# Carrying the second LayerNorm's transpose by VectorE blocks and SBUF transfers instead of TensorE, in an attention and feed-forward kernel

## Chip, cores and metric

One NeuronCore of one Trainium2 chip runs the whole program. The metric is the device time in microseconds (us) of one execution, and a lower time is better. A profiled execution of the same program gives the trace.

## The reference, cut to what matters

For each of 16 batches, `x` has 512 rows of 512 features and the context has 77 rows of 512.

```python
def block(x, ctx):
    h = layernorm(x)                                  # first LayerNorm
    sim = (h @ w1)[:, None] + (ctx @ w2)[None] + (h * w3) @ ctx.T + b
    hq = softmax(sim, axis=1) @ ctx
    hc = softmax(sim.max(axis=1)) @ h
    x = x + concat([h, hq, h * hq, h * hc]) @ W_qv + b_qv
    h2 = layernorm(x)                                 # second LayerNorm
    u = h2 @ W1 + b1
    q = u + (cos(th) * wr + sin(th) * wi) * wi * sin(th + 0.1 * u) * 0.1
    return x + relu(q) @ W2 + b2
```

`W1` is 512 x 2048 and `W2` 2048 x 512.

## The kernel before, in words

**Products.** Each fp32 matrix is held as a rounded high part and a low part, and each product is three matmuls (high x high, high x low, low x high; `three`, lines 500 to 502). A matmul of the feed-forward part has 128 partitions and 512 moving columns. `T[:, par]` holds the rows of one batch turned, so that features lie on the partitions: `T[:, par, 0]` is the high part, `T[:, par, 1]` the low part, each 4 chunks of features by 512 rows. The two values of `par` alternate from batch to batch.

**Order of the work.** The loop `body(b)` runs over 16 hidden tiles f = 0 to 15 of the feed-forward part of batch b and interleaves with them the attention of batch n = b + 1. All five engines have their own hand-written program with the same loop, and semaphores join them. On TensorE step f is `hidden(b, f)` (line 546, 12 matmuls into the PSUM tile `hid`) and then `second(b, f - 3)` (12 matmuls into `acc`). ScalarE reads `hid` in two passes (L846, L849), VectorE reduces the phase (L1168, L1170), ScalarE takes the sine (L859), VectorE adds it (L1160), and the ReLU is split into high and low parts (L855, L1174). Attention of the next batch: similarities in step 3, row and column maxima in steps 4 and 5, the turned probabilities in step 8, the products with `W_qv` in steps 10 and 11 (NA = 10). After these VectorE adds the result to `X` and takes the statistics of the second LayerNorm (`attention_and_stats`, line 1268), and GpSimd turns these into a reciprocal deviation (`deviation_second`, line 1552).

**The second LayerNorm's transpose.** In steps NA + 3 = 13 and NA + 4 = 14 the normalized rows are turned. `norm_second` (line 1276) on VectorE writes 128 rows to one of two buffers of `xin`; `tr_second` (line 599) on TensorE makes four 128 x 128 transposes through the identity into `mis` (L586, in `transpose_rows`, line 581); `turned_high` (line 764) on ScalarE rounds them from PSUM into the high part of `T`; `turned_low` (line 1065) on VectorE subtracts that from PSUM for the low part. `hidden(b + 1, 0)` waits for the last low part (`t2_lo`).

**The first LayerNorm's rows** come already turned from memory (`full`). The mean and deviation of each row are stored to DRAM and loaded back spread over the partitions (`spread_stats`, line 348, into `mean_bc` and `e_bc`); VectorE subtracts and multiplies (`center`, `scale`, L1047 and L1053), ScalarE and VectorE split the result (`spread_high`, `spread_low`, L771 and L1027).

**Queues.** SyncE issues the loads of inputs, the stores, `spread_stats` and `ctx_load` (line 381, seven transfers to `ctx_raw` and `tmp_w`), in program order. GpSimd issues the weight loads (512 KB each). In batch 0 the weights are split on the way and stored to DRAM, and later batches load them split, so in batch 0 ScalarE, VectorE and SyncE have more to do.

**The opening** (`attention_first` of each engine) splits `W_qv`'s second quarter, multiplies all context rows by it in ten groups (`rows_in`, `high_parts`, `low_part`, `multiply`, `product_add`, `product_out`), and works the attention of batch 0 between them. Its second LayerNorm is turned on TensorE too.

## Time and profile before

| what | us |
| --- | --- |
| median of 3 runs | 1970.97 (1969.54 to 1971.58) |
| the profiled execution, its own time | 1970.5 |
| its span in the trace | 1968.7 |
| TensorE busy | 1948.3 |
| VectorE busy | 1387.2 |
| ScalarE busy | 988.9 |
| GpSimd busy | 389.4 |

The span runs from the first instruction to the last in the trace, 1.8 us less than the execution's own time. In the rows a matmul's own duration is longer than the distance to the next one, since matmuls overlap; the distance between starts is what one costs. PE is TensorE, PEld its weight load, DVE VectorE, ACT ScalarE, POOL GpSimd, and SPq SyncE's DMA issues. A row with "x2" merges that many instructions. In square brackets, or behind a bar, stands the idle time before the instruction and what ended it. L12 is line 12 of the kernel before.

### The profile page before, as it was taken

Reading aid. Unit: us, or ns where it says so; the run is one execution under the profiler, and the core shown is the slowest. Engines: PE = TensorE matmul, PEld = TensorE weight load, DVE = VectorE, ACT = ScalarE, POOL = GpSimd, SP = SyncE. Lnnn points to the kernel's source line nnn. Section 1 sums busy time; section 2 is a strip of 40 time slices with the busy share of each in tenths; the row PEclk is TensorE's granted clock in tenths of the full one; section 3 lists DMA queues with packets and bytes.
Section 4 is the critical chain, followed back from the end, with each engine's and each line's share of the span. In section 5 each row is a group of like instructions: output and inputs, shape, how many; then the busy total and the mean of one; then the engine's idle time right before and its main releaser. Section 6 shows DMA issues by size and latency. Waiting matters only on the chain.

```text
span 1968.7 us, 24691 instructions
## 1 busy us (share of the span) xinstructions
PE 1948.3 (99%) x8807; PEld 1598.2 (81%) x8807; DVE 1387.2 (70%) x2405; ACT 988.9 (50%) x1676; POOL 389.4 (20%) x834
## 2 busy tenths in 40 slices
PE   8899999999999999999999999999999999999999
PEld 6678888888888888888888888888888888888887
DVE  6888776767777676776767767676776767767554
ACT  4574635536355363644636355363653636446343
POOL 1122212121211212112121211212112121121210
PEclk9999999999999999999999999999999999999999
DMA  8476947577474775747667485764747757476473
GB/s 247 166 266 240 291 145 224 182 212 222 152 224 144 243 220 160 237 145 222 203 189 226 138 236 166 225 221 155 232 134 242 222 166 231 146 221 181 146 216 119
DMA packets 140849, 391.73 MB, mean 199 GB/s; under 512 B 21876, under 2 KB 34856, under 8 KB 138808
## 3 DMA queue, kind: packets, MB, share of 16 engines
q0 software_dynamic: 83568, 304.29, 49.6%
q1 hardware_dynamic: 57016, 85.83, 14.0%
q8 instruction: 71, 1.16, 0.2%
q14 instruction: 50, 0.41, 0.1%
q10 hardware_dynamic: 144, 0.04, 0.0%
HBM read 351.83 MB, written 38.27 MB: 198 GB/s over the span
## 4 chain that ended last, share of the span: by engine, by line
PE 92%; DVE 3%; ACT 2%; DMA 1%; issue 1%; SPq 0%; DVEq 0%; ACTq 0%
PE acc L500 17%; PE acc L502 17%; PE acc L501 17%; PE hid L502 11%; PE hid L500 11%; PE hid L501 11%; PE mis L586 1%; PE acc L508 1%; PE acc L509 1%; PE mis L508 1%; PE mis L509 1%; PE mis L500 1%; PE mis L502 1%; PE mis L501 1%; DMA ph<-in_ctx_turned 1%
## 5 line engine op out<-in xcount | busy, mean ns | idle before, releaser
L500 PE MATMUL acc<-ws,act 128*128 128x512 f32 x1024 | 402.8, 393 | 1.7 <-DVE act L1174 1.7
L500 PE MATMUL hid<-T,w1s 128*128 128x512 f32 x1024 | 402.8, 393 | 0.4 <-ACT h L849 0.3
L502 PE MATMUL acc<-ws,act 128*128 128x512 f32 x1024 | 399.2, 390 | 0.0
L502 PE MATMUL hid<-T,w1s 128*128 128x512 f32 x1024 | 399.0, 390 | 0.0
L501 PE MATMUL acc<-ws,act 128*128 128x512 f32 x1024 | 398.7, 389 | 0.0
L501 PE MATMUL hid<-T,w1s 128*128 128x512 f32 x1024 | 398.7, 389 | 0.0
L1168 DVE TENSOR_SCALAR kk<-ph 128x512 f32<-128x512 f32 x256 | 108.8, 425 | 329.5 <-ACT ph L846 329.5
L855 ACT ACTIVATE act<-h 128x512 fp32r<-128x512 f32 x256 | 162.0, 633 | 351.7 <-DVE h L1160 330.3
L846 ACT ACTIVATE ph<-hid,hbias 128x512 f32<-128x512 f32 x256 | 175.8, 687 | 285.3 <-PE hid L502 285.0
L1509 POOL DMA_DIRECT2D ws<-w2x_dram x240 | 127.5, 532 | 556.2 <-PE acc L502 546.7
L1174 DVE SCALAR_TENSOR_TENSOR act<-h,act 128x512 fp32r<-128x512 f32 x256 | 176.0, 688 | 74.4 <-ACT act L855 73.1
L500 PEld LDWEIGHTS acc<-ws,act 128*128 128x128 f32 x1024 | 192.4, 188 | 41.7 <-DVE act L1174 2.5
L500 PEld LDWEIGHTS hid<-T,w1s 128*128 128x128 f32 x1024 | 192.3, 188 | 41.7 <-issue 1.2
L502 PEld LDWEIGHTS hid<-T,w1s 128*128 128x128 f32 x1024 | 192.2, 188 | 40.4
L502 PEld LDWEIGHTS acc<-ws,act 128*128 128x128 f32 x1024 | 192.2, 188 | 40.4
L501 PEld LDWEIGHTS acc<-ws,act 128*128 128x128 f32 x1024 | 192.4, 188 | 38.9
L501 PEld LDWEIGHTS hid<-T,w1s 128*128 128x128 f32 x1024 | 192.5, 188 | 38.7
L1503 POOL DMA_DIRECT2D w1s<-w1x_dram x240 | 129.6, 540 | 454.1 <-PE hid L502 442.1
L1160 DVE SCALAR_TENSOR_TENSOR h<-ph,camp,h 128x512 f32<-128x512 f32 x256 | 191.0, 746 | 0.0
L849 ACT ACTIVATE h<-hid,cols 128x512 f32<-128x512 f32 x256 | 174.6, 682 | 26.0 <-DVE act L1174 26.0
L1170 DVE TENSOR_TENSOR ph<-ph,kk 128x512 f32<-128x512 f32 x256 | 177.4, 693 | 8.8
L859 ACT ACTIVATE ph<-ph 128x512 f32<-128x512 f32 x256 | 158.3, 618 | 1.3 <-DVE ph L1170 1.0
(181 smaller groups left out, 2741.9 us busy)
## 6 DMA issues: line engine op xcount, KB each, us to landing
w1s<-w1x_dram POOLq DMA_DIRECT2D x240, 512.0 KB, 3.9
ws<-w2x_dram POOLq DMA_DIRECT2D x240, 512.0 KB, 4.6
ws<-wqx_dram POOLq DMA_DIRECT2D x56, 512.0 KB, 3.6
full<-in_x_turned SPq DMA_DIRECT2D x15, 1024.0 KB, 8.2
out_x<-X SPq DMA_DIRECT2D x15, 1024.0 KB, 4.7
X<-in_x SPq DMA_DIRECT2D x14, 1024.0 KB, 8.6
w_raw<-in_L_ffn_W SPq DMA_DIRECT2D x32, 256.0 KB, 3.8
w1x_dram<-w1s POOLq DMA_DIRECT2D x16, 512.0 KB, 4.0
```

The source lines that it names most:

```text
L500: pe.matmul(dst, w_hi, m_hi, start=start, stop=False)
L501: pe.matmul(dst, w_hi, m_lo, start=False, stop=False)
L502: mm = pe.matmul(dst, w_lo, m_hi, start=False, stop=stop)
L846: nc.scalar.activation(ph[:, f % 2], hid[:, f % 2], ACT.Identity, bias=hbias[:, f:f + 1], scale=HSCALE).then_inc(t_done, 1)
L849: nc.scalar.activation(h2[:, f % 2], hid[:, f % 2], ACT.Identity, bias=b1c[:, f:f + 1], scale=1.0).then_inc(h2_done, 1)
L855: nc.scalar.activation(act[:, f % 4, 0], h2[:, f % 2], ACT.Relu).then_inc(act_hi, 1)
L859: nc.scalar.activation(ph[:, f % 2], ph[:, f % 2], ACT.Sin, scale=TWO_PI_BELOW).then_inc(s_done, 1)
L1160: ve.scalar_tensor_tensor(out=h2[:, f % 2], in0=ph[:, f % 2], scalar=camp[:, f:f + 1], in1=h2[:, f % 2], op0=ALU.mult, op1=ALU.add).then_i ...
L1170: ve.tensor_tensor(ph[:, f % 2], ph[:, f % 2], kk[:], ALU.subtract).then_inc(r_done, 1)
L1174: ve.scalar_tensor_tensor(out=act[:, f % 4, 1], in0=h2[:, f % 2], scalar=0.0, in1=act[:, f % 4, 0].bitcast(F32), op0=ALU.max, op1=ALU.subtract
L1503: po.dma_start(w1s[:, s].rearrange("p a c k -> p (a c k)"), w1x_dram[f % FT].rearrange("p a c k -> p (a c k)")).then_inc(w1_in[s], 16)
L1509: po.dma_start(ws[:, slot_of(p)], tile_source(p, last, w2x_dram, wqx_dram)).then_inc(w_in[slot_of(p)], 16)
```

## The change

For the batches n = 1 to 15 the second LayerNorm's rows are no longer turned on TensorE. VectorE transposes each 128 x 512 tile in blocks of 32 x 32 into `ctx_raw` (`block_turn`, step 12, right behind each `norm_second`). SyncE then issues 16 transfers inside SBUF (`turned_blocks`, step 13), each 32 partitions by 2 KB, that carry the blocks to their partitions in the low half of `T`. ScalarE rounds them into the high half (`blocks_high`, step 14) and VectorE subtracts in place (`blocks_low`, start of step 15). The four groups i hold the rows 32i to 32i + 31 of each tile of 128, so `hidden` of batches 1 to 15 reads its moving operand in 16 runs of 32 columns (512 columns in all) and writes `hid` in the old order. Batch 0's own rows are turned as before.

Beside this: `spread_stats` and the reuse of `ctx_raw` by `ctx_load` stand behind the 16 transfers on SyncE; in the opening several steps of ScalarE, VectorE, SyncE and GpSimd change places; in batch 0's loop the first LayerNorm's split of batch 1 moves from steps 1 and 2 to steps 0 and 1, `g_high(1)` moves into the opening, and `add_b2` moves from steps 3 to 6 to steps 12 and 15.

```diff
 x2_done = sem("x2_done"); xb2_done = sem("xb2_done")
-st2 = sem("st2"); mo2 = sem("mo2"); rs2 = sem("rs2"); xn2 = sem("xn2"); tr2 = sem("tr2")
+st2 = sem("st2"); xb2 = sem("xb2"); t2_in = [sem(f"t2_in{i}") for i in range(4)]; mo2 = sem("mo2"); rs2 = sem("rs2"); xn2 = sem("xn2"); tr2 = sem("tr2")
...
+G = P // 32
+blocks = ctx_raw[:].rearrange("p a d -> p (a d)").rearrange("p (m c t r) -> p m c t r", m=G, c=C, t=RT)
+block_run = ctx_raw
+T_run = [T[:, q].rearrange("p a c r -> p a (c r)").rearrange("p a (i k) -> p a i k", i=G) for q in range(2)]
...
         sp.wait_ge(att_done, RT * n)
+        for i in range(G):
+            need(sp, t2_in[i], 16 * G * (n - 1))
...
         stack_load(n, hqw_raw, hqw_tail, hqw_dram, ctx_in)
+    def turned_blocks(eng, n, parts):
+        eng.wait_ge(xb2, RT * n)
+        for i in parts:
+            for m in range(G):
+                eng.dma_start(T_run[n % 2][32 * m:32 * m + 32, 1, i].bitcast(F32),
+                              block_run[32 * i:32 * i + 32, m]).then_inc(t2_in[i], 16)
...
         rows_in(7)
+        product_out(2)
+        rows_in(8)
...
         first_tile_load(1)
-        product_out(2)
-        rows_in(8)
...
                 continue
+            if f == NA + 3:
+                turned_blocks(sp, n, range(G))
...
                 turned_load(n + 1)
-            if f == (NA + 3 if first else NA + 2):
+            if f == NA + 4:
...
         for c in range(C):
-            three(hid[:, f % 2], w[:, 0, c], w[:, 1, c], T[:, par, 0, c], T[:, par, 1, c],
+            if b == 0:
+                m, dst = [T[:, par, k, c] for k in range(2)], hid[:, f % 2]
+            else:
+                m = [T_run[par][:, k, :, c * P:(c + 1) * P].rearrange("p i (t r) -> p t i r", t=RT) for k in range(2)]
+                dst = hid[:, f % 2].rearrange("p (t i r) -> p t i r", t=RT, i=G)
+            three(dst, w[:, 0, c], w[:, 1, c], m[0], m[1],
...
         pe.wait_ge(simt_done, n + 1)
+        need(pe, srow_done, n)
...
                 turn_stats(n + 1)
-            if f == NA + 3:
-                tr_second(n, 0)
-                tr_second(n, 1)
-            if f == NA + 4:
-                tr_second(n, 2)
-                tr_second(n, 3)
...
                        mis[:, t % 2].rearrange("p (c r) -> p c r", c=C)).then_inc(done, 1)
+    def blocks_high(n, i):
+        sc.wait_ge(t2_in[i], 16 * G * n)
+        nc.scalar.copy(T_run[n % 2][:, 0, i], T_run[n % 2][:, 1, i].bitcast(F32)).then_inc(t2_hi, 1)
...
         g_high(0)
-        context_high(0, range(0, 1))
...
             full_copy(0, t)
+        context_high(0, range(0, 1))
+        sim_bias(0)
         high_parts(6)
-        sim_bias(0)
+        row_exponentials(0)
         high_parts(7)
-        row_exponentials(0)
...
         product_copy(9)
+        g_high(1)
...
             g = FT * b + f
-            if f == 1 and not last:
+            if f == 1 and not first and not last:
...
                 continue
-            if f == 1:
+            if f == 0 and first:
+                for c in range(C):
+                    spread_high(n, c, pn)
+            if f == 1 and not first:
...
                     pr_high(n, c)
-            if f == NA + 3:
-                turned_high(n, 0, pn, tr2, t2_hi)
-                turned_high(n, 1, pn, tr2, t2_hi)
             if f == NA + 4:
-                turned_high(n, 2, pn, tr2, t2_hi)
-                turned_high(n, 3, pn, tr2, t2_hi)
+                for i in range(G):
+                    blocks_high(n, i)
...
+    def block_turn(n, t):
+        ve.wait_ge(xn2, RT * n + t + 1)
+        ve.transpose(blocks[:, :, :, t].rearrange("p m c r -> p c m r"),
+                     xin[:, t % 2].rearrange("p (c m r) -> p c m r", c=C, m=G)).then_inc(xb2, 1)
+    def blocks_low(n, i):
+        ve.wait_ge(t2_hi, RT * n + i + 1)
+        low(T_run[n % 2][:, 1, i], T_run[n % 2][:, 1, i].bitcast(F32), T_run[n % 2][:, 0, i]).then_inc(t2_lo, 1)
...
         if t >= 2:
-            ve.wait_ge(tr2, RT * n + t - 1)
+            ve.wait_ge(xb2 if n else tr2, RT * (n - 1) + t - 1 if n else t - 1)
...
     def add_b2(n, t):
-        ve.wait_ge(x2_done, RT * n + t + 1)
+        ve.wait_ge(x2_done if n else a_evac, RT * n + t + 1)
...
-        ve.wait_ge(xb2_done, RT * (b + 1))
+        need(ve, xb2_done if b else x2_done, RT * (b + 1))
...
-        if whole:
+        if whole or b == 0:
             ve.wait_ge(xb2_done, RT * (b + 1))
-        else:
+        if not whole:
...
             norm_first(t)
-        context_low(0, range(0, 1))
...
         turned_low(0, 3, 0, full_done, t1_lo)
+        low_part(5)
         sim_column(0)
-        low_part(5)
         product_add(2)
+        context_low(0, range(0, 1))
         product_add(3)
-        low_part(6)
...
         row_max(0)
-        low_part(7)
+        low_part(6)
...
         context_low(0, range(1, 2))
+        low_part(7)
...
                 chunk_low(n, 0)
-            if f == 2 and not last:
+            if f == 2 and not first and not last:
...
                 spread_low(n, 3, pn)
-            if f == NA + 3 and not last:
-                norm_second(n, 0)
-                norm_second(n, 1)
-            if f == NA + 4 and not last:
-                norm_second(n, 2)
-                norm_second(n, 3)
+            if f == NA + 5 and not last:
+                for i in range(G):
+                    blocks_low(n, i)
...
                 scale(n, 1)
+            if f == 0 and first:
+                g_low(n)
+                spread_low(n, 0, pn)
+                spread_low(n, 1, pn)
...
                 sim_column(n)
-                spread_low(n, 0, pn)
-                spread_low(n, 1, pn)
+                if first:
+                    spread_low(n, 2, pn)
+                    spread_low(n, 3, pn)
+                else:
+                    spread_low(n, 0, pn)
+                    spread_low(n, 1, pn)
...
                 center(n + 1, 1)
-            if first and 3 <= f < 3 + RT:
-                add_b2(b, f - 3)
+            if first and f in (NA + 2, NA + 5):
+                for t in range(2 * (f - NA - 2) // 3, 2 * (f - NA - 2) // 3 + 2):
+                    add_b2(b, t)
...
                 attention_and_stats(n)
-            if f == NA + 3:
-                turned_low(n, 0, pn, t2_hi, t2_lo)
-                turned_low(n, 1, pn, t2_hi, t2_lo)
-            if f == NA + 4:
-                turned_low(n, 2, pn, t2_hi, t2_lo)
-                turned_low(n, 3, pn, t2_hi, t2_lo)
+            if f == NA + 2:
+                for t in range(RT):
+                    norm_second(n, t)
+                    block_turn(n, t)
...
         po.wait_ge(s_w1q_lo, C)
-        po.wait_ge(c_tlo, 4)
+        po.wait_ge(c_tlo, 3)
...
         po.wait_ge(tr1, RT)
+        po.wait_ge(c_thi, GAP + 1)
         po.dma_start(w0_sb[:], wqv_dram[0]).then_inc(s_w0, 16)
-        po.wait_ge(c_tlo, GAP + 1)
+        po.wait_ge(c_tlo, GAP + 2)
```

## Rows read from the trace of the kernel before

**Rows 1.** Busy time of each engine over the whole span (the page).

```profile
PE 1948.3 (99%) x8807; PEld 1598.2 (81%) x8807; DVE 1387.2 (70%) x2405; ACT 988.9 (50%) x1676; POOL 389.4 (20%) x834
```

**Rows 2.** Chain that ended last, in order of time: start us, us, what.

```profile
309.05 0.88 PE mis L586 x8
...
1857.45 0.87 PE mis L586 x8
```

**Rows 3.** Timeline of TensorE around the first eight transposes of one batch: start us, us.

```profile
308.65 0.40 PE L502 MATMUL acc<-ws,act 128*128 128x512 f32 x1
...
310.00 0.40 PE L501 MATMUL hid<-T,w1s 128*128 128x512 f32 x1
310.23 0.39 PE L502 MATMUL hid<-T,w1s 128*128 128x512 f32 x1
```

**Rows 4.** Waits of TensorE up to 200 us: total us, times, longest us.

```profile
PE mis L500 <- DVE T L1027: 4.6, 1, 4.6
PE acc L500 <- DVE act L1027: 3.7, 2, 1.9
PE mis L615 <- ACT tmp_w L864: 1.9, 1, 1.9
PE acc L500 <- DVE act L1174: 1.7, 2, 1.0
```

**Rows 5.** Groups of instructions over the span: busy us, mean ns of one | idle before.

```profile
L1027 DVE TENSOR_TENSOR T<-full,T 128x512 fp32r<-128x512 f32 x60 | 38.5, 682 | 0.0
...
L771 ACT CAST T<-full 128x512 fp32r<-128x512 f32 x60 | 34.0, 614 | 17.3 <-DVE full L1053 17.3
...
L1280 DVE TENSOR_SCALAR xin<-X,mv,rstd 128x512 f32<-128x512 f32 x64 | 32.0, 543 | 1.6 <-PE mis L586 1.6
L586 PEld LDWEIGHTS mis<-ident,xin 128*128 128x128 f32 x256 | 29.7, 140 | 4.7 <-issue 0.7
...
L622 PEld LDWEIGHTS mis<-ident,rmax 128*128 128x128 f32 x64 | 8.1, 139 | 2.2 <-issue 0.2
```

**Rows 6.** Timeline of VectorE, loop steps 12 to 15 of batch 1.

```profile
299.41 1.00 DVE L1280 TENSOR_SCALAR xin<-X,mv,rstd 128x512 f32<-128x512 f32 x2
307.08 0.43 DVE L1168 TENSOR_SCALAR kk<-ph 128x512 f32<-128x512 f32 x1 [6.68 <-ACT ph L846]
...
321.49 2.36 DVE L1047 TENSOR_TENSOR full<-full,mean_bc 128x1024 f32<-128x1024 f32 x2
```

**Rows 7.** Timeline of ScalarE, loop step 14 of batch 1.

```profile
316.33 1.05 ACT L766 CAST T<-mis 128x512 fp32r<-128x512 f32 x2
```

**Rows 8.** Timeline of SyncE's DMA issues, batch 1.

```profile
303.90 0.32 SPq L351 DMA_DIRECT2D stat_dram<-mean_bc  x1
305.82 0.34 SPq L355 DMA_DIRECT2D mean_bc<-stat_dram  x1
...
308.26 0.27 SPq L376 DMA_DIRECT2D ctx_raw<-in_ctx  x1
```

**Rows 9.** DMA issues: KB each, median us from issue to landing.

```profile
X<-in_x SPq DMA_DIRECT2D x14, 1024.0 KB, 8.6
...
e_bc<-stat_dram SPq DMA_DIRECT2D x15, 256.0 KB, 6.8
```

**Rows 10.** Timeline of TensorE: first matmul of the next batch, batches 1 and 0.

```profile
321.55 0.39 PE L500 MATMUL hid<-T,w1s 128*128 128x512 f32 x1
...
202.13 0.39 PE L500 MATMUL hid<-T,w1s 128*128 128x512 f32 x1
```

**Rows 11.** Timeline of SyncE, loop step 13 of batch 0.

```profile
192.29 0.40 SPq L351 DMA_DIRECT2D stat_dram<-mean_bc  x1
```

**Rows 12.** Timelines of ScalarE at 31 us and TensorE at 96 us.

```profile
30.89 0.62 ACT L793 CAST act<-ph 128x512 fp32r<-128x512 f32 x1 [6.14 <-DMA ph<-in_ctx_turned]
...
96.35 0.63 PE L502 MATMUL mis<-T,gs 128*77 128x512 f32 x1
```

**Rows 13.** Stretch 90 to 100 us: us, busy of each engine (x), PEclk, DMA share, GB/s.

```profile
90.00:100.00 10.00, 5.38 (x15) 3.16 (x14) 7.99 (x17) 7.46 (x16) 1.75 (x4) 0.68 0.55 191
```

## The prediction

> **What bounds the kernel now.** I read the busy times first: TensorE is busy 99% of the span, VectorE 70%, ScalarE 50% [rows 1]. So what leaves TensorE's queue shortens the run, and other engines count only where they make it wait. In the chain that ended last the work is periodic: the first group of eight transposes of `xin` (L586) of batch 1's loop stands at 309.05 and that of batch 14's, 13 batches on, at 1857.45 us, so a batch takes (1857.45 - 309.05) / 13 = 119.11 us [rows 2]. The view of waits lists none for TensorE after the first loop; the large ones are in the opening and that loop [rows 4]. In that steady state the time of a batch is the sum of what TensorE issues.
>
> **The removed transposes.** The last matmul ahead of a group of eight starts at 308.65, and the second one behind it at 310.00: 1.35 us, where two steps of 0.23 (310.00 to 310.23) would be usual [rows 3]. A group costs 1.35 - 0.46 = 0.89 us. There are two groups a batch in 15 batches: 30 x 0.89 = **26.7 us** come off TensorE's path. The casts and subtractions of before (ScalarE 2.1 us, VectorE 2.6 us a batch) are replaced by as many on SBUF at 614 and 682 ns [rows 5], so only the block transposes are new work.
>
> **Is the new path in time?** I follow batch 1. TensorE wants the turned rows at 321.55 [rows 10]; with 2 x 0.89 gone that is 319.8.
> - VectorE. Its first `norm_second` is at 299.41, two of them in 1.00 [rows 6]. A block transpose has no row. Its bounds are 0.54 us (one input, 128x512, as `xin`) and 1.37 us (twice the 682 ns of a subtraction) [rows 5]; I take 0.68, one element a cycle as the subtraction. A pair with its hand-over is 0.5 + 0.7 = 1.2 us, four are 4.8, ready at 304.2. The cover is the idle 6.68 us ahead of 307.08 [rows 6]; if it were gone VectorE would be 2.7 us a batch busier, of 119. The slow end gives 4 x 1.87 = 7.5 us, ready at 306.9, still inside it.
> - What the skill says against this: the Trainium skill (VectorE: DVE Perf Modes, The three transpose paths) gives 390 ns for a 128x128 bf16 transpose on TensorE and 311 ns on VectorE, and advises TensorE for a whole 128x128. By its VectorE figure a tile of four would take 1.24 us, an estimate from that page, with the blocks ready 2.2 us later; by its TensorE figure the 240 transposes would be 94 us, and the forecast some 67 us lower than mine. The trace does not agree with that price: eight cost 0.89 us of the path, 0.11 each [rows 3].
> - SyncE. Issuing takes it 0.27 us for a small piece (L376) and 0.32 to 0.34 for the others [rows 8]; the bounds for one step are thus 0.3 and, with a gap as long again, 0.6. At 0.42, 16 take 6.7 us, 304.3 to 311.0. A row for a landing of 16 small ones is missing. Nearest: a 1 MB load with the same 2 KB pieces lands in 8.6 us [rows 9], so all could have landed at 312.9; the lone 6 KB store took 1.9 (303.90 to 305.82) [rows 8], and `e_bc` 6.8 in the same crowd [rows 9]. So the last lands between 311.0 + 1.9 = 312.9 and 311.0 + 6.8 = 317.8. I take 314.
> - ScalarE starts its casts behind the sine of step 14, before at 316.33 [rows 7], now 315.4. Four at 0.55 end at 317.6; the last one needs its data at 317.05. VectorE's last subtraction ends 0.7 later, 318.4. TensorE has 1.4 us to spare then, and a landing up to 317.05 costs nothing: together 4.4 us of slack behind 314.
> - `spread_stats` on SyncE stands behind the transfers: store at 311.1 instead of 303.90, loads at 313.0 and 313.4, `e_bc` landed at 320.2 (with 6.8) [rows 8, 9]. `center` stood at 321.49 [rows 6], now due at 319.7 + 0.4 for the subtractions ahead of it = 320.1. VectorE may wait some tenths, which its idle time in the next steps takes up. `ctx_load` then comes 8 us later, at 315, and its first readers stand in step 1 of the next loop, 11 us after 321.55: free.
>
> So the steady state keeps the whole 26.7.
>
> **The first loop.** In step 13 of batch 0, SyncE first waits to reload the weight buffers; only at 192.29 is it free [rows 11]. The 16 transfers then run to 199.0 and land by 202 (taking the 3 us of above). Cast and subtraction of the last group add 1.3, 203.3. TensorE wants them at 202.13 - 1.78 = 200.35 [rows 10]: a wait of 3 us. `e_bc` of batch 2 comes at 199.5 + 0.5 + 2.5 + 6 = 208.5, so `center` waits, and the low ReLU part that `second` needs behind it is ready some 2 us late; catching up and a slower clock add about 1.5. I price the first hand-over at **+6.5 us**; its ends are 0 (SyncE reaches the transfers earlier) and 10.
>
> **The opening.** Three things. (1) ScalarE stood 6.14 us in front of a context load that landed at 30.89 [rows 12] with `sim_bias` queued behind it, and TensorE waited 1.9 us for that (L615); the other of the two waits for `act` L1027 was 3.7 - 1.9 = 1.8, for a split that stood behind `hqs` [rows 4]. The new order takes `sim_bias` first and `hqs` later. Both waits together are 3.7, and the slower matmuls behind the first about 1 more: 4.5. What is late next is `w0`: it waits for the context group that landed at 30.89 and needs 8.6 us for 1 MB [rows 9], so it comes at 39.5 at the latest. (2) The 4.6 us wait for `T` ahead of `sim` [rows 4]: VectorE's two subtractions (2 x 0.62) and `g_low` (0.4) move a step forward and the phase work of a step (1) no longer stands ahead of them, 2.6 us. The eleven matmuls behind that wait last 0.63 instead of 0.39 us [rows 12, 3], so they go some 0.2 slower each, 2.2 in all: the granted clock is 0.68 over these 10 us [rows 13], full clock (2.4 GHz) and its half mixed. A shorter wait gives back perhaps 1 of it. `g_high(1)` waits for `ctx_in` and may take a part back. About 3.5. (3) `add_b2` out of steps 3 to 6 lets the ReLU parts come earlier; the waits for them are 1.7 us [rows 4]: 1. Together **-9 us**, between 0 and -14.
>
> **Sum.** -26.7 + 6.5 - 9 = -29.2 against the profiled execution's 1970.5 (span 1968.7 and 1.8 around it), which is 0.5 under the median 1970.97: 1941.3, or 1941.8 against the median. I say **1941.5 us**.
>
> **The rivals.**
> - *The blocks land late in every batch.* With more than 4.4 us over my landing TensorE waits in all 15; from 320.2 on (314 + 4.4 + 1.78) the gain is gone. For it: the DMA engines are crowded there, `e_bc` takes 6.8 us [rows 9]. Against it: the seven `ctx_load` transfers leave this stretch. With a typical wait of 1 us: 1941.5 + 15 = 1956. Chance 0.13.
> - *Slower than before: the broken moving operand costs time.* `hidden` of batches 1 to 15 reads 16 runs where it read one, in 15 x 192 = 2880 matmuls. Gain and cost meet at 29.2 / 2880 = 10 ns, 0.63 ns a run, 1.4 columns (0.23 us / 512 = 0.45 ns). At two columns a run: 14.4 ns a matmul, +41 us, 1941.5 + 41 = 1982. At half rate it would be +650. For it: no moving operand of before is broken. Against it: TensorE's weight loads from a broadcast column (`rmax`) take 139 ns and from plain rows 140 [rows 5], so its reads don't mind a step. Chance 0.06.
> - *The opening gives nothing and the first loop costs its 6.5.* For it: ScalarE and VectorE are dense there, and each wait removed uncovers the next. 1941.5 + 9 = 1950.5. Chance 0.13.
> - *The first hand-over is hidden too.* 1935. Chance 0.08.
>
> **How the numbers follow.** The forecast has 0.60, with a range of its own of 1934 to 1949 for the opening's bounds. Adding most of the late blocks and both opening cases: 1931 to 1958. Left out are the slower case and the worst of the late blocks. A measurement of this kernel can tell 0.2%, 4 us. Faster by more: 0.60 + 0.13 + 0.08 + 0.11 of the late blocks = 0.92; within it 0.02; slower 0.06, the broken operand.
>
> **What would show it.** In the profile after: 16 transposes of `xin` on TensorE where 256 were; a period of 119.11 - 1.78 = 117.33 us; matmuls into `hid` still 0.23 apart; 60 block transposes of 128x512 near 0.68 us each; 240 transfers on SyncE, the last of a batch landing before ScalarE's fourth cast; no wait of TensorE on `T` from batch 1 on, and one of some 3 us at 200 us less the opening's gain; the wait ahead of `sim` near 2 us. A period above 117.6, or `hid` matmuls more than 0.23 apart, makes the forecast wrong.

## The result, and the profile after

The changed kernel takes 2033.9 us (median of 4 runs, 2030.0 to 2042.2) beside 1970.3 us (4 runs) of the kernel before: a ratio of 1.0331, 95% interval 1.0318 to 1.0345. It is 63.6 us slower where the forecast was 29.5 faster, and it lies outside the range. The profiled execution has a span of 2034.9 us.

The page of the changed kernel: busy times (which answer to [rows 1]), and the groups of matmuls into `hid` (busy us, mean ns | idle before).

```profile
PE 1964.3 (97%) x8567; PEld 1574.8 (77%) x8567; DVE 1428.8 (70%) x2465; ACT 993.8 (49%) x1676; POOL 390.9 (19%) x834
...
L517 PE MATMUL hid<-T,w1s 128*128 128x512 f32 x1024 | 408.8, 399 | 26.1 <-DVE T L1049 21.8
...
L519 PE MATMUL hid<-T,w1s 128*128 128x512 f32 x1024 | 406.4, 397 | 0.0
```

TensorE has 240 instructions less and is busy 16 us longer, and its idle time grew from 1968.7 - 1948.3 = 20.4 to 2034.9 - 1964.3 = 70.6 us. So there are two losses: one in its own work, one in waits. The timeline of TensorE shows the first (beside [rows 3]; start us, us):

```profile
425.17 0.40 PE L517 MATMUL hid<-T,w1s 128*128 128x512 f32 x1
...
427.97 0.39 PE L517 MATMUL acc<-ws,act 128*128 128x512 f32 x1
```

From 425.17 to 427.97 twelve matmuls into `hid` take 2.80 us, 0.2333 each, where the usual step is 0.2267: 6.6 ns more, on 2880 of them (6.2 against the mean step of before, 0.2272). The waits of TensorE, and those of VectorE on transfers (total us, times, longest):

```profile
PE mis L517 <- DVE T L1049: 24.5, 14, 3.1
PE hid L517 <- DVE T L1049: 21.8, 13, 10.8
...
DVE full L1069 <- DMA e_bc<-stat_dram: 43.1, 14, 4.5
DVE e_bc L1174 <- DMA ctx_raw<-hqw_dram: 13.8, 8, 3.2
```

`hid` <- `T` is the hand-over of the turned rows; `mis` <- `T` is `sim` of the next batch, which [rows 4] has once and now 14 times. What makes them late is in SyncE's issues in the loop of batch 2, with the blocks of batch 3 (they answer to [rows 8]; start us, us), and in ScalarE's casts:

```profile
437.11 10.97 SPq L408 DMA_DIRECT2D T<-ctx_raw  x16
448.13 0.55 SPq L356 DMA_DIRECT2D stat_dram<-mean_bc  x1
453.61 0.34 SPq L360 DMA_DIRECT2D mean_bc<-stat_dram  x1
```

```profile
452.70 0.62 ACT L788 CAST T<-T 128x512 fp32r<-128x512 f32 x1 [2.50 <-DMA T<-ctx_raw]
...
462.38 0.69 ACT L870 ACTIVATE h<-hid,cols 128x512 f32<-128x512 f32 x1 [4.42 <-DVE act L1196]
```

The 16 issues take 11.0 us, 0.69 each, and the last cast starts 452.70 - 437.11 = 15.6 us behind the blocks. The store of the statistics, issued behind them, needs 5.5 us to land (448.13 to 453.61; 3.2 to 6.3 over the loops of batches 1 to 13) where [rows 8] has 1.9. So `center` on VectorE starts late, and with it all that feeds the next `sim`. VectorE and then TensorE:

```profile
436.37 0.71 DVE L1301 STREAM_TRANSPOSE ctx_raw<-xin 128x512 f32<-128x512 f32 x1
...
459.38 2.36 DVE L1069 TENSOR_TENSOR full<-full,mean_bc 128x1024 f32<-128x1024 f32 x2 [3.61 <-DMA e_bc<-stat_dram]
```

```profile
476.02 0.43 PE L517 MATMUL mis<-T,gs 128*77 128x512 f32 x1 [2.11 <-DVE T L1049]
...
477.23 0.63 PE L519 MATMUL mis<-T,gs 128*77 128x512 f32 x1
477.66 0.63 PE L517 MATMUL mis<-T,gs 128*77 128x512 f32 x1
```

There is a second way to the same wait. The context loads, behind the statistics on SyncE, land late too. In the loop of batch 5 the last of them takes 15.4 us (the chain's row, then VectorE's, then TensorE's):

```profile
827.85 15.42 DMA ctx_raw<-hqw_dram
```

```profile
843.29 0.69 DVE L1174 CUSTOM_DVE_ANT_0 e_bc<-ctx_raw,w_bc 77x512 f32<-77x512 f32 x1 [3.22 <-DMA ctx_raw<-hqw_dram]
```

```profile
847.72 0.42 PE L517 MATMUL mis<-T,gs 128*77 128x512 f32 x1 [3.14 <-DVE T L1049]
...
850.29 0.40 PE L519 MATMUL mis<-T,gs 128*77 128x512 f32 x1
```

This is the longest wait ahead of `sim`. VectorE waits for the statistics in all 14 loops and for the context in eight. The stretch at 477 us again, in windows (us, busy of TensorE (x), PEclk, DMA share, GB/s):

```profile
465.00:474.00 9.00, 8.91 (x39) 1.00 0.75 236
474.00:477.00 3.00, 0.98 (x5) 1.00 0.57 158
477.00:481.00 4.00, 4.00 (x12) 0.57 0.14 48
481.00:486.00 5.00, 5.00 (x25) 1.00 0.64 223
```

Behind the wait of 2.11 the matmuls go 0.43 apart instead of 0.23. The granted clock over 477 to 481 us is 0.57, so for most of it the lower of its two levels (1.2 GHz), and 1.00 before and behind. TensorE was busy throughout before the wait and idle in it. Seven steps at 0.2 us more are 1.4 us, two thirds of the wait itself. That is not so behind every wait: in this trace the lower level follows five of the 14 waits ahead of `sim`, and behind the longest, of 3.14, the granted clock is 1.00 and eleven steps take 2.57 us, 0.234 each.

The period, from the chain that ended last: the store of the statistics stands at 448.13 and, 11 batches on, at 1803.59, so (1803.59 - 448.13) / 11 = 123.22 us, where it was 119.11 [rows 2] and 117.33 was forecast.

### The profile page after: what moved, and what is told of

The parts are those of the page before. It is cut to its first block, busy times and chain, and to the rows that moved or that the text cites. A ratio compares the mean times of both kernels' runs of the same rounds, so it can differ in the third digit from the quotient of the medians.

```text
span 2034.9 us, 24495 instructions
## 1 busy us (share of the span) xinstructions
PE 1964.3 (97%) x8567; PEld 1574.8 (77%) x8567; DVE 1428.8 (70%) x2465; ACT 993.8 (49%) x1676; POOL 390.9 (19%) x834
## 4 chain that ended last, share of the span: by engine, by line
PE 59%; DVE 11%; DMA 10%; SPq 9%; ACT 6%; issue 5%; ACTq 0%; DVEq 0%
PE acc L519 12%; PE acc L518 12%; PE acc L517 11%; SPq L408 7%; PE hid L517 6%; PE hid L518 6%; PE hid L519 6%; DMA ctx_raw<-hqw_dram 3%; DMA stat_dram<-mean_bc 3%; DMA e_bc<-stat_dram 2%; DVE h L1182 1%; DVE xin L1312 1%; DVE T L1049 1%; DVE ph L1192 1%; DVE full L1075 1%
## 5 line engine op out<-in xcount | busy, mean ns | idle before, releaser
L517 PE MATMUL hid<-T,w1s 128*128 128x512 f32 x1024 | 408.8, 399 | 26.1 <-DVE T L1049 21.8
L519 PE MATMUL hid<-T,w1s 128*128 128x512 f32 x1024 | 406.4, 397 | 0.0
L518 PE MATMUL hid<-T,w1s 128*128 128x512 f32 x1024 | 406.2, 397 | 0.0
L517 PEld LDWEIGHTS acc<-ws,act 128*128 128x128 f32 x1024 | 192.6, 188 | 57.5 <-DVE act L1196 15.4
```

The lines of the kernel that those rows point to most:

```text
L517: pe.matmul(dst, w_hi, m_hi, start=start, stop=False)
L518: pe.matmul(dst, w_hi, m_lo, start=False, stop=False)
L519: mm = pe.matmul(dst, w_lo, m_hi, start=False, stop=stop)
```

## The experiments

Three questions: what the 16 runs cost, what the transfers cost and through which step, and what the opening gives. In the short diffs "after" is the changed kernel.

**Price of the runs, by itself.** The kernel before, with `hidden` of batches 1 to 15 reading the same 512 elements in pieces; the order of the elements (with 4 runs also their choice) is another from batch 1 on, and nothing else is left out.

```diff
-three(hid[:, f % 2], w[:, 0, c], w[:, 1, c], T[:, par, 0, c], T[:, par, 1, c],
+m = [T[:, par, k, c].rearrange("p (i t r) -> p t i r", i=4, t=4) for k in range(2)]   # i=8, t=8: 64 runs
+dst = hid[:, f % 2].rearrange("p (t i r) -> p t i r", i=4, t=4)
+three(dst, w[:, 0, c], w[:, 1, c], m[0], m[1],
```

> The kernel before, whose hidden matmuls of batches 1 to 15 read the same 512 moving columns as 16 runs of 32 (so the columns come in another row order and the output differs in that). Nothing else changes. Theory A (each run of the moving operand costs one column's time, about 0.41 ns): 6.6 ns more between starts, 0.2267 to 0.233 us, 2880 matmuls, +19 us, about 1989. Rival B (the slower matmuls of the changed kernel come from the block transfers and the other traffic in SBUF): 0.2267 as before, 1970.

Measured: 1994.2 us, ratio 1.0125 (1.0109 to 1.0140), 24.2 us more. The timeline of TensorE in that kernel has the changed kernel's pitch, with no wait beside it:

```profile
305.04 0.40 PE L502 MATMUL hid<-T,w1s 128*128 128x512 f32 x1
...
307.14 0.40 PE L502 MATMUL hid<-T,w1s 128*128 128x512 f32 x1
307.37 0.39 PE L500 MATMUL acc<-ws,act 128*128 128x512 f32 x1
...
308.76 0.39 PE L500 MATMUL acc<-ws,act 128*128 128x512 f32 x1
```

Nine steps from 305.04 to 307.14 are 2.10 us, 0.2333 each. That is theory A, at this number of runs: the pitch is the one it forecast, and rival B, the traffic of the transfers, is out, since there is none. The period confirms it: the store of the statistics stands at 305.05 and 12 batches on at 1753.37, 120.69 us, 1.58 above before. Between 300 and 1800 us the mean step of a `hid` matmul is 233.4 ns beside 227.2 before, which is 1.2 us a batch. The other 0.4 lies in `second` behind it, though its own operands are whole: 229.4 ns beside 227.2 in the mean. In the rows above its first six steps, 307.37 to 308.76, take 1.39 us, and six usual ones 1.36. Why is open.

With 4 runs of 128 (`T_run[par][:, k, :, c * P:(c + 1) * P]`, the changed kernel's layout without its inner step) and with 64 runs of 8, one execution each:

> As b_runs16, with 4 runs of 128 columns taken 512 columns apart. Theory A (a price per run): 1.7 ns a matmul, +5 us, about 1975. Rival C (a fixed price for any broken operand): 6.6 ns, +19 us, about 1989.

> As b_runs16, with 64 runs of 8 columns. Theory A (a price per run): 26.7 ns a matmul, +77 us, about 2047. Rival C (a fixed price): +19 us, about 1989.

Measured: 1970.7 us with 4 runs (no cost to be seen, the mean of a `hid` matmul is 394, 390 and 390 ns by line, as before) and 2054.8 us with 64. The group of `hid` with 64 runs:

```profile
L502 PE MATMUL hid<-T,w1s 128*128 128x512 f32 x1024 | 430.5, 420 | 0.0
```

By the time, a matmul costs 24.2 / 2880 = 8.4 ns more with 16 runs and 85 / 2880 = 29 ns more with 64, about half a nanosecond a run, near one column's 0.44; and nothing at 4, where theory A had 5 us and rival C 19. So neither theory holds over the whole range. Number and length of the runs change together here, and which of the two counts is not separated. The Trainium skill (SBUF — State Buffer, Specifications (TRN2), the row on cachelines) asks for at least two accesses in each 16-byte line for full bandwidth. Runs of 128 and of 32 bytes use their lines as fully as one long run does, so by that rule neither would cost more than it. The runs decide against it here.

**The changed kernel with one run.**

```diff
-m = [T_run[par][:, k, :, c * P:(c + 1) * P].rearrange("p i (t r) -> p t i r", t=RT) for k in range(2)]
-dst = hid[:, f % 2].rearrange("p (t i r) -> p t i r", t=RT, i=G)
+m, dst = [T[:, par, k, c] for k in range(2)], hid[:, f % 2]
```

> The changed kernel, but hidden reads the turned rows of batches 1 to 15 in the order in which they lie, as one run of 512 (the rows of a batch then come out in another order). Theory R (the 16 runs cost 6.6 ns a matmul wherever they are read): the pitch of the matmuls into hid goes from 0.2333 back to 0.2267 and 2880 x 6.6 ns = 19 us go, 2034 - 19 = 2015; if the waits of TensorE stay as long, that is all. Rival W (TensorE only reaches its waits sooner, because the transfers set the time of a batch): 2025 to 2034, with the waits ahead of sim and hid longer by as much. Rival V (the pitch comes from something else in the changed kernel): pitch still 0.2333, 2034.

Measured: 2023.6 us, ratio 1.0283 (1.0266 to 1.0300), 10.3 us under the changed kernel. The group and the waits:

```profile
L519 PE MATMUL hid<-T,w1s 128*128 128x512 f32 x1024 | 401.5, 392 | 0.0
```

```profile
PE hid L517 <- DVE T L1048: 24.7, 13, 9.8
PE mis L517 <- DVE T L1048: 24.6, 13, 2.4
```

The mean falls from 397 to 392 ns, but less than half of the 24.2 us comes back. R and W each hold in part. By the pages of the two profiled executions, 13.7 us apart, TensorE is busy 20.9 us less (1943.4 beside 1964.3) and idle 7.2 more (77.8 beside 70.6): the matmuls are short again, and TensorE only reaches some of its waits sooner. The lower clock takes a part too; it is granted in seven loops behind the first here, in five in the changed kernel.

**Without the transfers.** Block transposes, casts and subtractions stay; the 16 transfers go, and `hidden` reads one run. The second half of each batch from batch 1 on therefore works on what lay in `T`.

```diff
-if f == NA + 3:
-    turned_blocks(sp, n, range(G))
...
-sc.wait_ge(t2_in[i], 16 * G * n)
+sc.wait_ge(xb2, RT * n)
```

> The changed kernel without the 16 transfers a batch and with one run of 512: VectorE still turns the blocks, ScalarE casts and VectorE subtracts four pieces (of what lies in T already, so the second half of each batch from batch 1 on works on other numbers). Theory T (transfers and runs are all that went wrong; the removed transposes are worth 26.7 us): 1970.3 - 26.7 - 4.5 of the opening + 0 to 3 for the first hand-over = 1939 to 1942, period of a batch 117.3 us, no waits ahead of sim. Rival W (VectorE's 60 block transposes, 0.71 us each, push sim's split and center back by themselves): waits ahead of sim of 1 us or more remain, period over 118, 1955 or more.

Measured: 1941.7 us, ratio 0.9860 (0.9845 to 0.9874). Two stores of the statistics, 12 batches apart, give (1708.84 - 300.93) / 12 = 117.33 us:

```profile
300.93 0.32 SPq L356 DMA_DIRECT2D stat_dram<-mean_bc  x1
...
1708.84 0.32 SPq L356 DMA_DIRECT2D stat_dram<-mean_bc  x1
```

Theory T holds and rival W is out: VectorE's block transposes cost nothing, and the removed groups are worth what the forecast gave them. All that was lost lies in the transfers and the runs.

**The order on SyncE.** The changed kernel with the statistics ahead of the transfers, and then with half of the transfers on GpSimd:

```diff
 if f == NA + 3:
+    if n + 1 < B:
+        spread_stats(n + 1)
     turned_blocks(sp, n, range(G))
```

> The changed kernel (2033.9) with spread_stats ahead of the 16 transfers on SyncE, as in the kernel before. Theory S (the loads of mean and deviation behind the transfers are what makes VectorE and then TensorE wait): VectorE's 43 us of waiting for e_bc go, TensorE's 24.5 us in front of sim and the slower clock behind them go, the transfers come about 3 us later and TensorE's wait for the turned rows grows from 0.8 to 2 or 3 us a batch: about 2010. Rival L (issue and landing of the transfers are the bound, whatever stands behind them): the wait for the turned rows grows by as much as the other shrinks, 2030 or more.

Measured: 2079.6 us, ratio 1.0556 (1.0539 to 1.0574). That is rival L's side, and worse than it: theory S had about 2010. The wait for `e_bc` is gone and so is that ahead of `sim`, but the transfers start 2.8 us behind the blocks (ready at 442.25), because SyncE sits out the landing of the store (441.93 to 443.90) and then issues the two broadcasts. The last cast stands 20.7 us behind the blocks instead of 15.6, so beside the later start some 2.2 us are slower landings, behind the broadcasts. All of it lands on `hid`:

```profile
PE hid L517 <- DVE T L1049: 84.6, 15, 12.8
...
ACT T L788 <- DMA T<-ctx_raw: 103.0, 48, 8.2
```

```profile
441.93 0.32 SPq L356 DMA_DIRECT2D stat_dram<-mean_bc  x1
443.90 0.34 SPq L360 DMA_DIRECT2D mean_bc<-stat_dram  x1
...
445.02 11.14 SPq L408 DMA_DIRECT2D T<-ctx_raw  x16
```

On one queue the statistics and the blocks stand in each other's way: whichever comes second is late. Here TensorE waits 4.3 to 6.5 us in 13 of the hand-overs behind the first (the last has 1.0), and the lower clock sets in during or right behind each of these 13.

```diff
-            turned_blocks(sp, n, range(G))            # SyncE: m in range(G)
+            turned_blocks(sp, n, range(G), range(2))  # SyncE: m in range(2)
+# GpSimd, at the start of step NA + 3
+po.wait_ge(xb2, RT * n)
+for i in range(G):
+    for m in range(2, G):
+        po.dma_start(T_run[n % 2][32 * m:32 * m + 32, 1, i].bitcast(F32),
+                     block_run[32 * i:32 * i + 32, m]).then_inc(t2_po[i], 16)
```

> The changed kernel with half of the 16 transfers of a batch issued by GpSimd instead of SyncE. Theory I (the queue that issues them, 16 x 0.65 us, sets when the last one lands): SyncE issues 8 in 5.5 us, GpSimd the other 8 beside it, the last cast stands 4 to 5 us earlier, e_bc with it, TensorE's waits of 1.1 and 1.9 us a batch go, with the slower clock behind them: 15 x 3 to 4.5 us less, 1968 to 1990. Rival E (the DMA engines, 16 x 32 pieces of 2 KB and their landing, set it): last cast at most 1 us earlier, 2020 to 2034. Rival G (GpSimd's issues are slower and hold up its weight loads): slower than 2034.

Measured: 2062.9 us, ratio 1.0476 (1.0454 to 1.0498). Theory I holds for the blocks. For the time G came true in its second half only: GpSimd's issues are not slower (0.50 us in the median beside SyncE's 0.59), but they do hold up its weight loads. SyncE's and GpSimd's issues:

```profile
436.19 4.99 SPq L409 DMA_DIRECT2D T<-ctx_raw  x8
```

```profile
436.47 1.03 POOL L1636 DMA_DIRECT2D T<-ctx_raw  x2 [7.18 <-DVE ctx_raw L1303]
437.71 2.94 POOL L1636 DMA_DIRECT2D T<-ctx_raw  x6 [0.20 <-issue]
440.64 0.58 POOL L1541 DMA_DIRECT2D w1s<-w1x_dram  x1
```

All 16 are issued in 5.0 us instead of 11.0, and the wait of `hid` on `T` is down to 8.5, once. But GpSimd stood 7.18 us at the blocks with its weight loads queued behind them, and then issued seven of 512 KB in 4.2 us (440.64 to 444.88). The store of the statistics, issued at 441.23, takes 5.5 us to land, behind eight transfers as behind 16, and SyncE's context loads behind it stick, one of them already at its issue (3.9 us at 451.62). VectorE waits for `ctx_raw<-hqw_dram` 67.4 us in 13 times (13.8 in the changed kernel), and TensorE ahead of `sim` 60.0 instead of 24.5. That the bunch of weight loads is what holds them is a reading of these rows; the next kernel changes it together with the place of the store.

**Both faults mended.** GpSimd's half comes one step later (NA + 4), behind the weight loads of step 14; SyncE issues the store of the statistics first, then its 8 transfers, and the broadcasts behind them, when the store has landed.

```diff
+def store_stats(n):
+    sp.wait_ge(srow_done, n)
+    sp.dma_start(stat_dram[n % 2], srow).then_inc(stat_st, 16)
 def spread_stats(n):
-    sp.wait_ge(srow_done, n)
-    sp.dma_start(stat_dram[n % 2], srow).then_inc(stat_st, 16)
     sp.wait_ge(stat_st, 16 * n)
...
+if n + 1 < B:
+    store_stats(n + 1)
 turned_blocks(sp, n, range(G), range(2))
```

> The changed kernel with half of the 16 transfers on GpSimd, but one step later in its program (behind the weight loads of step 14, so that none of them waits for the blocks), and with SyncE's store of the statistics ahead of its 8 transfers and the two broadcasts behind them. The 16 runs stay. Theory I (the issuing queue sets the last landing, and in the run with half on GpSimd the weight loads held up there crowded the context loads): no wait of TensorE above 1 us a batch, period 117.33 + 1.27 for the runs = 118.6, time 1970.3 - 26.7 - 4.5 + 19 = 1958 to 1965. Rival E (the DMA engines are too full for the blocks and the context at the same time): waits ahead of sim remain, 1990 or more.

Measured: 1975.3 us, ratio 1.0027 (1.0014 to 1.0039): 58.6 us less than the changed kernel, 10 above theory I's upper end; rival E is out. Two waits of TensorE above 2.3 us are left, both in batch 0, and SyncE's issues in the loop of batch 2 follow each other as meant:

```profile
PE hid L524 <- DVE T L1057: 10.1, 1, 10.1
PE hid L524 <- ACT h L878: 4.0, 1, 4.0
```

```profile
429.55 0.32 SPq L356 DMA_DIRECT2D stat_dram<-mean_bc  x1
429.91 5.15 SPq L412 DMA_DIRECT2D T<-ctx_raw  x8
435.16 0.61 SPq L363 DMA_DIRECT2D mean_bc<-stat_dram  x1
```

SyncE's broadcasts now go out at once behind its transfers, 5.6 us behind the store. By the pages of the two profiled executions TensorE is idle 42.8 us less than in the changed kernel (27.8 beside 70.6) and busy 17.4 less (1946.9 beside 1964.3), the latter in part the clock. In batch 0's loop the mending does little: 16 issues took 13.9 us there in the changed kernel, and eight still take 10.3 (5.6 in the median of the later loops):

```profile
187.74 13.91 SPq L408 DMA_DIRECT2D T<-ctx_raw  x16
```

```profile
188.22 10.30 SPq L412 DMA_DIRECT2D T<-ctx_raw  x8
```

Theory I had 1958 at its low end; the excess of 17 is about what the other experiments give for the first hand-over (11 to 13) and for the runs above the 19 assumed (5). How the 58.6 divide between the two changes was not tried here; the last pair below gives 20.6 for the second queue, which leaves some 38 for the store's place, an estimate.

**And one run again, by a stage.** The transfers land in `prs`, which is free then, and the casts and subtractions, which had to run anyway, write `T` in the old order of the rows. The second `g_high`, which the change had put into the opening, is back in the first loop.

```diff
-eng.dma_start(T_run[n % 2][32 * m:32 * m + 32, 1, i].bitcast(F32),
+eng.dma_start(stage[32 * m:32 * m + 32, i].bitcast(F32),
...
-nc.scalar.copy(T_run[n % 2][:, 0, i], T_run[n % 2][:, 1, i].bitcast(F32)).then_inc(t2_hi, 1)
+nc.scalar.copy(T_nat[n % 2][0][:, i], stage_nat[:, i].bitcast(F32)).then_inc(t2_hi, 1)
```

> As the run before it, and the transfers land in a stage (the tile prs, free at that time) and not in T; ScalarE's casts and VectorE's subtractions write T in the old order of the rows, so that hidden reads one run of 512 again. The second g_high, put into the opening, is back where it was. Theory: runs and late blocks both gone, casts and subtractions as long as before; 1970.3 - 26.7 - 4.5 + 0 to 5 for the first hand-over = 1939 to 1945, below the kernel before. Rival: writing 32 elements at a time makes casts (0.61 us) and subtractions (0.68 us) longer; at twice the time VectorE and ScalarE are 2.5 us a batch later and sim's split waits: 1950 to 1975. Rival E as above: 1970 or more.

Measured: 1953.2 us, ratio 0.9907 (0.9892 to 0.9922), faster than the kernel before, though above the theory's 1945. Writing 32 elements at a time is free on both engines (ScalarE, then VectorE, mean ns beside 614 and 682 of [rows 5]):

```profile
L794 ACT CAST T<-prs 128x512 fp32r<-128x512 f32 x60 | 33.0, 613 | 10.7 <-DMA prs<-ctx_raw 10.7
```

```profile
L1056 DVE TENSOR_TENSOR T<-prs,T 128x512 fp32r<-128x512 f32 x60 | 37.8, 686 | 14.3 <-ACT T L794 14.3
```

Against the run before it, 22.1 us are gone, and this time the whole price of the runs: by the pages TensorE is busy 23.4 us less (1923.5 beside 1946.9) and idle as long as before (28.0 beside 27.8). The second `g_high` gave nothing on balance: the wait on `h` is 1.4 instead of 4.0, but a wait of 2.4 for `gs` ahead of `sim` has come. The one long wait left is that of 9.7 us at the first hand-over.

**The first hand-over on TensorE, and one queue.** In batch 0 `tr_second`, `turned_high` and `turned_low` stay as before; transfers from batch 2 on. The second kernel is the first with all 16 transfers on SyncE.

```diff
+if first and f == NA + 3:
+    tr_second(n, 0)
+    tr_second(n, 1)
+if first and f == NA + 4:
+    tr_second(n, 2)
+    tr_second(n, 3)
```

> As c_best2 (stage, old order of rows, transfers from two queues, store of the statistics first), but the rows of batch 1 are turned by TensorE as in the kernel before, in steps 13 and 14 of batch 0; transfers only from batch 2 on. Theory H (what c_best2 lacks to 1942 is the first hand-over, a wait of 9.7 us and the slower clock behind it): two groups of eight transposes come back, 1.8 us, the wait goes: 1953.2 - 9.7 - 1 + 1.8 = 1944 to 1946, period 117.3. Rival: the wait moves to batch 1's own hand-over or to sim behind it, 1950 or more.

> c_best3 with all 16 transfers on SyncE, between the store of the statistics and the two broadcasts; nothing on GpSimd. Theory I (16 x 0.65 us of issuing set the last landing, 2.8 us after the time by which ScalarE's last cast would need it): the wait of 1 to 2.8 us a batch comes back at hid, with a slower clock behind it, 14 batches: 14 to 45 us above c_best3, about 1970. The context and e_bc come later than in c_best3 too, so that sim may wait. Rival J (what made the changed kernel slow was e_bc and the statistics behind the transfers, and that is cured by the store ahead of them): within 4 us of c_best3.

Measured: 1942.2 us, ratio 0.9855 (0.9838 to 0.9873), and 1962.7 us, ratio 0.9967 (0.9956 to 0.9978). H holds, a little under its 1944. The one-queue kernel decides for theory I against J: 20.6 us are lost again when eight issues a batch return to SyncE. It stays under the kernel before all the same, with the store ahead of the transfers. With one queue, the waits of TensorE and ScalarE:

```profile
PE hid L529 <- DVE T L1069: 13.9, 12, 2.4
...
ACT T L801 <- DMA prs<-ctx_raw: 31.3, 19, 2.5
```

With two queues TensorE's list has no wait of `hid` on `T` of a microsecond or more, and ScalarE never waits for `prs<-ctx_raw`. The Trainium skill (DMA: Bandwidth & Descriptors, Issuing engines are not separate DMA queues) says that issuing from several engines saves only the issuing time, "which is usually small relative to the DMA itself". The first half agrees: the gain is issuing time, 16 issues in 10.7 us on one queue against 5.7 us on two in one and the same loop, while the transfers themselves land no sooner (4.5 us in the median on one queue; 5.5 on SyncE's and 4.7 on GpSimd's of two). The second does not apply to pieces of 64 KB: each issue takes 0.6 us, and 16 of them take more than twice as long as one landing.

**The opening alone.** The kernel before with only the new order of the opening and of batch 0's loop.

> The kernel before with only the new order of the opening and of the first loop (no block transposes, no transfers, one run). If only the first of the three terms holds (the wait for sim_bias): 1970.3 - 4.5 = 1965.8. If all three hold as forecast: 1961. If each wait removed uncovers the next: 1970.

Measured: 1966.8 us (10 executions), ratio 0.9988 (0.9979 to 0.9998): 2.9 us, small but clear of 1. The first matmul on `w1s` stands at 74.19 us instead of 79.10, 4.9 earlier; term (1) is there and a little larger. The wait ahead of `sim`, of 4.6, is gone too, but in its place TensorE waits 4.0 us on ScalarE's `h` ten microseconds behind the opening:

```profile
PE hid L513 <- ACT h L867: 4.0, 1, 4.0
```

The changed kernel has the same wait (4.2 us), and its chain leads from there through ScalarE's four splits of `g_high(1)` back to a context load:

```profile
72.11 8.79 DMA ctx_raw<-hqw_dram
80.92 1.49 ACT tmp_w L834 x4
```

The forecast had named that ("may take a part back") and gave it next to nothing.

## Why the prediction was wrong

What held: the value of the removed groups (1.78 us a batch; without transfers the period is 119.11 - 1.78 = 117.33), the block transposes (0.712 us, taken as 0.68), the blocks ready 4.8 us behind the first `norm_second` (432.26 to 437.08), VectorE's cover, and casts and subtractions as cheap as before. What failed, in the order of size:

1. **"At 0.42, 16 take 6.7 us".** The rows of single issues, 0.27 to 0.34, were the wrong neighbours: none is of a transfer inside SBUF of 32 pieces of 2 KB. It measured 0.69 a piece, above the upper bound of 0.6, and 13.9 us in batch 0. The landing behind it (about 4.5 us in the median) was in the bounds. Together the last cast came 15.6 us behind the blocks. By the forecast it needed its data 317.05 - 304.2 = 12.85 behind them, and TensorE had 1.4 us to spare then: the slack was overdrawn by 15.6 - 12.85 - 1.4 = 1.35 us, and TensorE waited 1.1 us at `hid` in this batch (0.9 in the mean of the twelve waits behind the first). So the forecast's account of the slack was right and the issue time put into it was not.
2. **"VectorE may wait some tenths".** `spread_stats` behind the transfers was priced by the issues alone, as a store landing in 1.9 us. The store goes out 4.1 us later than forecast, lands in 5.5 behind 16 transfers, and `center` waits 3.6; ScalarE's `h`, VectorE's splits and `sim` are late in turn, 24.5 us of waiting. "`ctx_load` then comes 8 us later [...]: free" failed with it: VectorE waits for the context in eight loops, and the longest wait of `sim` comes that way. In five loops the slower clock adds to it. Points 1 and 2 together are the 58.6 us between the changed kernel and the one with mended queues. The rival "late in every batch" had the mechanism, and its 1 us a batch is the size of the wait at `hid`; it did not know the larger one ahead of `sim`, nor the clock.
3. **"So its reads don't mind a step".** This argued from a weight load with a fixed step to a moving operand with 16 runs, which is another operand and another shape. Break-even was worked out rightly, at 0.63 ns a run; the price is about 0.5, so alone it would have taken back 24 of the 29 us. The chance of 0.06 was far too small for a cost with no row at all, and the two rivals were priced as if only one could come true.
4. **The first hand-over at +6.5.** TensorE waited 10.8 us, not 3, since SyncE's 16 issues took 13.9 us there instead of 6.7. Halving them did not cure it: with mended queues eight took 10.3 us and the wait was still 10.1. Between the kernel with the stage and the one that also turns batch 1's rows on TensorE it measures 11.0, and 1.8 for the two groups that come back: 12.8.
5. **The opening at -9** gave 2.9: the first of its three terms came in full, and the rest was taken back. (Its stated bounds, 0 to -14, give 1936 to 1950.5, not quite the range of 1934 to 1949 that was set "for the opening's bounds".)

The sum of the parts, as measured one after another: 2033.9 less 58.6 (queues), less 22.1 (runs and second `g_high`), less 11.0 (first hand-over) is 1942.2. That this is close to the 1941.5 of the forecast is chance: the forecast was for the changed kernel, and another first hand-over and opening stand behind its number.

Open: why an issue of this kind takes 0.6 to 0.7 us and up to 1.3 in batch 0's loop; why `second` slows down behind a `hidden` that reads 16 runs; why the clock falls behind some waits and not behind others as long.

## What to carry to other kernels

Where work goes from a compute engine to small transfers, count issues times the issue time of a transfer of the same shape, and look at what already stands on that queue: the order store, pieces, loads lets the pieces hide the store's landing. Look also at what stands behind the pieces on that queue, down to loads that seem to have ten microseconds to spare. Two issuing engines help, if the second one does not have to wait there with other loads behind it. A layout that breaks a matmul's moving operand into many runs is paid in each matmul that reads it; if a copy is on the way anyway, let the copy put it straight.

## What the runs showed of the hardware

- A matmul of 512 columns, whose step is 0.2267 us, costs nothing more with 4 runs of its moving operand, 8.4 ns more with 16 and 29 ns more with 64; of the 8.4, 6.2 are in its own mean step and 2.2 in those of the matmuls behind, whose operands are whole.
- Casts on ScalarE (613 ns) and subtractions on VectorE (686 ns) that write 128 x 512 in runs of 32 take what they take with plain rows.
- VectorE's transpose of 128 x 512 fp32 in 32 x 32 blocks takes 712 ns.
- SyncE's issue of a 64 KB transfer inside SBUF takes 0.59 us in the median and 0.51 to 1.8 in the changed kernel; GpSimd's, with half of them there, 0.50 in the median and 0.50 to 0.69.
- A 6 KB store behind 16 such transfers on SyncE lands in 3.2 to 6.3 us (loops of batches 1 to 13), ahead of them (the statistics first on the queue) in 1.3 to 3.0.
- A wait of 2.1 us on TensorE was followed by a stretch with a mean granted clock of 0.57, which cost 1.4 us; a wait of 3.1 us in the same trace was followed by full clock.
